# Splits on GpSimd behind the pair's last addition, second products three experts behind, and sums behind the second unit

## What is computed

```python
x = x + _L0_xattn_ref(_layernorm(x), ctx_768, Wq, Wk, Wv, Wo, bo)
x = x + _L0_ffn_ref(_layernorm(x), router_w, router_b, sw1, sb1, sw2, sb2, rw1, rb1, rw2, rb2)

# attention
attn = softmax(einsum('bhsd,bhld->bhsl', q, k) * DIM_HEAD ** -0.5)
out = einsum('bhsl,bhld->bhsd', attn, v).transpose(0, 2, 1, 3).reshape(B, S, INNER) @ Wo + bo

# experts
router_probs = softmax(flat @ router_w + router_b)
topk_probs, topk_idx = top_k(router_probs, 2)
weights = zeros_like(router_probs).at[arange(T)[:, None], topk_idx].add(topk_probs)
shared_out = gelu(flat @ sw1 + sb1) @ sw2 + sb2
h1 = gelu(einsum('td,edh->teh', flat, rw1) + rb1[None])
expert_out = einsum('teh,ehd->ted', h1, rw2) + rb2[None]
mixed = einsum('ted,te->td', expert_out, weights)
return shared_out + mixed
```

## Time and profile before

| | |
|---|---|
| three runs | 444.71, 444.64, 442.39 us; median 444.64 |
| profiled execution | 444.56 us, span 442.6 us |
| mean granted TensorE clock | 0.992 |
| PE busy | 430.1 us (97%) |
| DVE busy | 284.3 us (64%) |
| POOL busy | 265.5 us (60%) |
| ACT busy | 220.0 us (50%) |
| chain that ended last, by engine | PE 83%, POOL 8%, issue 4%, DVE 3%, ACT 2% |

### The profile page before, as it was taken

The page is one execution under the profiler, slowest core; times in us unless marked ns, Lnnn a source line. Parts: engine busy times, 40 slices in busy tenths (PEclk is TensorE's granted clock), DMA queues, the critical chain, the costliest instruction groups (busy, mean ns, idle before and its releaser), DMA issues.

```text
span 442.6 us, 7246 instructions
## 1 busy us (share of the span) xinstructions
PE 430.1 (97%) x2526; PEld 333.3 (75%) x2526; DVE 284.3 (64%) x551; ACT 220.0 (50%) x384; POOL 265.5 (60%) x180
## 2 busy tenths in 40 slices
PE   9999999989899999999999999999999999999996
PEld 7787777667587878687868786878786776776885
DVE  4785878787555769684348597843486775547443
ACT  3555444215275336263754352637333844786773
POOL 4629995919368485673684865736445710667771
PEclk9999999969999999999999999999999999999999
DMA  7400002000000020000000300000000000000000
GB/s 227 132 1 2 1 2 57 0 2 0 2 0 2 0 57 1 2 2 0 1 1 1 89 21 2 1 2 0 2 0 2 1 1 1 0 1 1 25 1 24
DMA packets 13994, 7.37 MB, mean 17 GB/s; under 512 B 9308, under 2 KB 12936, under 8 KB 13960
## 3 DMA queue, kind: packets, MB, share of 16 engines
q1 hardware_dynamic: 13960, 6.92, 6.3%
HBM read 6.36 MB, written 0.52 MB: 16 GB/s over the span
## 4 chain that ended last, share of the span: by engine, by line
PE 83%; POOL 8%; issue 4%; DVE 3%; ACT 2%; ACTq 0%; POOLq 0%; DVEq 0%
PE ps L1216 17%; PE ps L1130 11%; PE ps L1200 10%; PE ps L1201 10%; PE ps L1202 10%; PE ps L1042 7%; PE ps L1044 6%; PE ps L1043 6%; POOL work L543 4%; POOL g_lo L728 2%; PE ps L1084 2%; PE ps L1050 1%; PE ps L1142 1%; DVE work L545 1%; POOL ctxT_lo L651 1%
## 5 line engine op out<-in xcount | busy, mean ns | idle before, releaser
L804 ACT ACTIVATE probs<-ps 128x512 f32<-128x512 f32 (+1 forms) x208 | 123.9, 598 | 143.9 <-PE ps L1202 136.9
L930 DVE TENSOR_REDUCE maxes<-ps 128x1 f32<-128x402 f32 x256 | 131.9, 566 | 53.6 <-PE ps L1130 53.4
L543 POOL TENSOR_TENSOR work<-work,probs 128x1024 f32<-128x1024 f32 x54 | 128.9, 2386 | 15.9 <-ACT probs L804 13.0
L1216 PE MATMUL ps<-probs,v_sb 128*64 128x256 f32 (+1 forms) x832 | 93.4, 381 | 0.8 <-ACT probs L804 0.8
L541 POOL TENSOR_TENSOR work<-probs 128x1024 f32<-128x1024 f32 x14 | 33.5, 2390 | 98.2 <-issue 69.9
L1216 PEld LDWEIGHTS ps<-probs,v_sb 128*64 128x64 f32 (+1 forms) x832 | 59.1, 137 | 34.1 <-ACT probs L804 4.9
L1200 PE MATMUL ps<-g_hi,ctxT_hi 97*128 97x512 f32 (+1 forms) x208 | 83.7, 402 | 0.0
L1201 PE MATMUL ps<-g_lo,ctxT_hi 96*128 96x512 f32 (+1 forms) x208 | 82.7, 398 | 0.0
L1202 PE MATMUL ps<-g_hi,ctxT_lo 96*128 96x512 f32 (+1 forms) x208 | 82.3, 396 | 0.0
L1130 PE MATMUL ps<-ctxT_hi,g_hi 96*128 96x402 f32 x256 | 73.6, 362 | 0.4 <-DVE maxes L930 0.3
L728 POOL TENSOR_TENSOR g_lo<-probs,g_hi 128x512 fp32r<-128x512 f32 x32 | 40.7, 1294 | 35.1 <-ACT g_hi L826 33.9
(11 more groups left out here) (149 smaller groups left out, 537.9 us busy)
## 6 DMA issues: line engine op xcount, KB each, us to landing
raw<-in_ctx_T_dram SPq DMA_DIRECT2D x3, 600.4 KB, 4.4
work<-in_L_ffn_rw_dram SPq DMA_DIRECT2D x1, 1024.0 KB, 7.5
g_hi<-neg_row SPq DMA_DIRECT2D x60, 0.5 KB, 2.0
raw<-in_ctx_T_dram SPq DMA_DIRECT2D x3, 150.8 KB, 3.0
x_sb<-in_x_dram SPq DMA_DIRECT2D x1, 384.0 KB, 6.1
early<-in_WqkT_dram SPq DMA_DIRECT2D x1, 336.0 KB, 4.5
wo_sb<-in_L_xattn_Wo_dram SPq DMA_DIRECT2D x1, 256.0 KB, 5.1
out_dram<-x_sb SPq DMA_DIRECT2D x1, 256.0 KB, 2.2
```

Source lines behind the costliest of these rows:

```text
L543: ops.tensor_tensor(acc, acc, pr, ALU.add).then_inc(summed, 1)
L804: nc.scalar.activation(probs[0:rows, n % SLOTS, j, :], s_bank(chunk_no(*w))[0:rows, :], ACT.Exp, scale=SCALE).then_inc(probs_ready, 1)
L930: v.tensor_reduce(maxes[:, p % 2, i * T + t, blk:blk + 1], src[:, 0:BW], AX.X, ALU.max).then_inc(ring_taken, 1)
L1216: ins = mm(o_bank[DH * i:DH * (i + 1), :], v_sb[0:rows, c, h * DH:(h + 1) * DH], probs[0:rows, n % SLOTS, j, i * S:(i + 1) * S], start=(c ...
```

## The change

There are four edits. `added(b, p)` makes GpSimd wait until all six additions of a pair are counted in `summed`, and is put ahead of its context splits, `w1` splits, the bias addition, the `b2` split and the powers. The sums and quotients of pair 0 move from behind units 3 and 4 of pair 1 to behind units 1 and 2. LAG is 3 instead of 2, and the end of the list of the expert phase is written anew. REST_0 is 3 instead of 8.

```diff
-REST_0 = 8
+REST_0 = 3
...
-LAG = 2
+LAG = 3
...
-                if n and (u, j) in (((4, 0), (4, 1)) if n == 1 else ((0, 1), (1, 1))):
-                    main.append(("quotient", order[n - 1] + ((u, j) in ((4, 1), (1, 1)),)))
-            if (n, u) == (1, 3):
+                if n and (u, j) in (((2, 0), (2, 1)) if n == 1 else ((0, 1), (1, 1))):
+                    main.append(("quotient", order[n - 1] + ((u, j) in ((2, 1), (1, 1)),)))
+            if (n, u) == (1, 1):
                 main.append(("sums", order[0]))
...
     rest = [i for new in waiting for i in new]
-    out += [("second", (i, 0)) for i in rest] + [("out", (last, 0))]
-    out += [("second", (i, 1)) for i in rest[:-chunks]] + [("ring", ("back", last, 0))]
-    out += [("second", (i, 1)) for i in rest[-chunks:]]
+    known, newest = rest[:-chunks], rest[-chunks:]
+    out += [("second", (i, 0)) for i in known] + [("second", (i, 1)) for i in known[:-chunks]]
+    out += [("second", (i, 0)) for i in newest] + [("out", (last, 0))]
+    out += [("second", (i, 1)) for i in known[-chunks:]] + [("ring", ("back", last, 0))]
+    out += [("second", (i, 1)) for i in newest]
...
+            def added(b, p):
+
+                pool.wait_ge(summed, (b * PAIRS + p + 1) * (NU - 1))
+
             for kind, w in steps:
                 if kind == "ctx":
+                    added(w[0] - 1, int(w[0] == 1))
                     low_part(*w)
...
                 if kind == "scores" and w == (0, 3, NU - 1, 0):
 
+                    added(0, 3)
...
                 if kind == "scores" and w == (1, 2, NU - 1, 0):
+                    added(1, 2)
...
                     pool.wait_ge(s_w1, 32)
+                    added(0, 2 * w)
                     then_own(g.tensor_copy(w1_hi[:, es], w1_sb[:, es]))
...
                 if kind == "roots":
+                    if w + 1 < B:
+                        added(w + 1, 1)
                     inverse_roots(slice(w * T, w * T + T), B + w + 1)
```

## The result

The changed kernel takes 440.34 us in the median of 7 runs (437.86 to 440.66), the kernel before, run on the same chip, 444.64 (7 runs, 442.39 to 445.29): a ratio of 0.9897, 95% interval 0.987 to 0.9924. That is 1.0% faster. The forecast was 434.1 us, its range ended at 438.8. The profiled execution took 440.66 us (span 438.9); against the 444.56 of the one before, 3.9 us were gained of the 10.5 forecast.

A forecast was written before the change was run, and what follows sets the result against it. TensorE, busy 97% of the span, was taken as the bound, leaving idle time, half-clock stretches and needless work. 0.7 + 1.2 + 2.4 + 3.1 + 2.0 + 1.1 = 10.5 us off 444.56 gave 434.1 us, range 431.8 to 438.8.

The forecast's parts named there:

- the steps for pairs 2 and 3 and for the clock: Row sums: holding GpSimd's split removes waits of 2.4 us (pair 2) and 2.0 (pair 3), and 3.1 of slow clock.
- The tight cover of pair 3: End of pair 3: VectorE done 20.1 us after pair 2's sums, TensorE's values 20.3, so 0.2 us early; 2.0 at stake.
- the 1.2 us of pair 1: Pair 1: earlier quotient and sums of pair 0 plus GpSimd's waits gain 1.2 us; at least 0.8 by the quotient alone.
- the 0.7 of the start: Start: five dummy products less let the transposes start 0.74 us sooner, taken as 0.7; bounds 0 and 0.75.
- The third expert of delay: Expert phase: second products three experts behind, net 1.1 us gained; 2.1 at best, 0.3 lost at worst.
- rival B: Experts: the new 2.0 us wait for xn brings the clock down, a 6.8 us fall costing 3.1: 437.2 us; chance 0.22.
- a case in which it would take 0.2: Routing weights' chain: VectorE's cast takes 0.2 us instead of 1.20, and the experts give 2.1 us instead of 1.1.
- a second gap of 1.6: Expert phase: TensorE waits 1.6 us for the routing weights, there at 401.3 while they come at about 403.0.
- The end: Last products: one expert's seconds more (1.4 us) cover the 1.7 us of waits on the last splits to about 0.2.
- C: Pairs 3 or 2: GpSimd's additions rule once TensorE is fast, 1 to 2 us of waiting stay: 435.6 us; chance 0.12.
- D: Last additions are slow for another reason than GpSimd; only 0.7 + 0.8 + 1.1 remain: 442.0 us; chance 0.04.
- E: Ends of nine pairs: GpSimd becomes the bound, its 1.5 us holds reaching the next additions, 13.5 us more: 447.6 us; chance 0.03.

The follow-up runs named there:

- e9: The kernel before with only GpSimd's waits on the pair's last addition (`added` and its calls): 435.79 us, ratio 0.9812.
- e1: The changed kernel with the experts' edit undone (second products two experts behind, old end of the list): 436.53 us, ratio 0.9814.
- e2: The kernel before with only the experts' edit (second products three experts behind, new end of the list): 448.76 us, 1.0% slower.
- e8: e5 with eight dummy products at the start instead of three: ratio 0.9762 to the kernel before.
- e5: The changed kernel with GpSimd's 14th split of activations held until VectorE has written the last routing weights: 434.86 us.
- e7: The changed kernel with eight dummy products at the start instead of three: ratio 0.9865 to the kernel before.
- e6: The changed kernel with second products two experts behind in the first half of the tokens, three from the second half on: 434.14 us.
- e11: The kernel before with three dummy products at the start instead of eight, nothing else: ratio 1.000.
- e12: e6 with eight dummy products at the start instead of three: 434.25 us, ratio 0.9775 to the kernel before.
- e13: e12 with GpSimd's 14th split of activations held until the routing weights are written: 434.35 us.
- e14: The changed kernel with 12 dummy products of 128x512 on TensorE ahead of the transposes of the routing weights only: 436.41 us.

## Why the prediction was wrong

**Attention and start.** Right in the profile: 9.4 us forecast, 9.4 measured at the first split. The waits on the last addition gave what the steps for pairs 2 and 3 and for the clock said (7.5; e9, with its part of pair 1, 8.4 by its ratio). The tight cover of pair 3 held as worked out: from pair 2's sums VectorE was done after 20.2 us and TensorE with its values after 20.4 (20.1 and 20.3 forecast). Counted without the start the gain is 8.6 us, of 8.7 forecast. Two small terms were put to the wrong edit or were luck: the 1.2 us of pair 1 measured 1.0, and the waits make nearly all of it, while at least 0.8 was given to the quotient; the 0.7 of the start holds in the profiled execution (0.87) and not in the median. The prediction also took the quick run of 442.39 us for one perhaps without the fall. The later quick runs of this kernel, at 442.44 and 442.55, have a granted clock of 0.996 against 0.992 in most: about half the time at the low clock, not none.

**The third expert of delay.** This is the step that failed: a gain of 1.1 us forecast, a loss of 5.5 in the profile, 3.7 and 4.3 in the runs of e1 and e2. Of the 5.5 us 5.2 stand up to the last products; the rest is the transfer behind them, 3.5 us instead of 3.0, and that differs between executions of the same code as well (3.0 in e8, 4.6 in e5). Its walk of TensorE was right up to the transposes of xn (387.4 on the old axis; 378.01 + 9.43 = 387.44, after a wait of 2.0). Then three things came that the sum did not hold:

- The clock fell behind the gap of 2.0 us. This was rival B. Its fall was 3.3 and not 6.8 us long and cost 3.3 x 0.45 = 1.5 us; it made the router 0.9 us late instead of 0.6 to 0.7 early. In e7, where this fall did not come, the router is 0.67 us early, as forecast.
- The weights' chain got longer by 2.1 us. The prediction kept the cast at 1.20 us and named a case in which it would take 0.2. It looked at the one instruction whose row was slow, and only for a gain. The copy and the subtraction behind it had taken 0.2 each because the splits happened to be over; in the new order GpSimd had six splits in a row, and both took 1 us more. The wait for the weights was 3.8 instead of 1.6 us. e7 has the same 3.8 us in a profile without the first fall, so it is this chain and not the late router that makes it.
- The clock fell in that wait. Of the 6.7 us at half clock TensorE worked 5.9, which cost 5.9 x 0.45 = 2.7 us. Rival B had asked this only of the 2.0 us gap; the sum had a second gap of 1.6 and never asked what it would do to the clock if it came out longer.

1.5 + 2.1 + 2.7 = 6.3 us, against a miss of 6.6. The first two also put the weights where they were measured: at 397.03 + 9.43 = 406.5, 3.5 us after the forecast 403.0. No rival held more than the first of the three, so the range ended at 438.8.

**The end.** Right: seconds of one expert more cover the last splits. It is the 1.8 us of e6, which has them without the price, and the 2.2 us of e5 and e8.

**The rivals.** B came, with a smaller price, behind the gap that it named. Its argument, that the clock had not fallen behind the gap of 1.97 us, was one execution's luck: it fell there in e2 and e11 (last section). C, D and E did not come: no wait on GpSimd's additions in pairs 2 and 3, additions at 0.69 us, and GpSimd's held instructions never in front of an addition that was due.

The versions that keep the gains are e6, e8, e12 and e13, at 433.9 to 434.4 us, and e5 at 434.9; their intervals overlap and none can be called the best. All beat both kernels.

## What to carry to other kernels

Work that is put off leaves a hole in front of the next wait: before an order is changed, follow each chain that TensorE will meet earlier, and price the gap together with the clock that may fall in it. A chain of small VectorE instructions on the critical path has a short length beside an idle GpSimd (0.6 us for these three) and a long one if each meets a busy one (3.7); price it at the long one if the change can make GpSimd's stretch longer, and if it matters, hold GpSimd while the chain runs (0.8 us in e5). The delay may differ by place: short where the chain is awaited, long where it covers the end.

## What the hardware showed that was not expected

- The same gap does not always bring the clock down. Behind the gap of 2.0 us the changed kernel's profile has a fall and the profiles of e5, e7, e8 and e14 have none; and of e7's six runs one has a granted clock of 1.0, though its order leaves a gap of 3.8 us. Such a fall can be 3.3 us or 6.7 us long. The kernel before has a fall behind pair 2 and none behind pair 3's gap of 1.97 us; e2, the same code there, has a fall behind both (1.99 us in pair 3), and e11 one in pair 3 alone, behind 1.91 us:

```profile
113.69 0.72 PE L1084 MATMUL ps<-work,ones 128*64 128x256 f32 x4 [1.91 <-DVE work L546]
...
114.20:120.90 6.70, 6.70 (x18) 5.31 (x17) 2.19 (x4) 2.13 (x4) 0.00 (x0) 0.50 0.01 4
```

- The kernel with twelve dummy products of 0.235 us in the gap (e14) is 3 us faster than without them; about 2 us of that is the clock, the rest a shorter chain.
- At the start the same code had the spacing of the full clock from near 4 us in one execution and only after 9.2 in another.
- The same last transfer ended the span 3.0 us after the last transposes in one profile and 4.6 in another (e8, e5).
